# Layer norm issued inside the chunk, K evacuation on ScalarE, and per-tile waits in the first down projection of a retention + mixture-of-experts layer

## The reference, cut to what matters

```python
# attention half (retention): no softmax, a decay mask per head
xn = layernorm(x)                               # (8, 4096, 1024)
Q, K, V = (einsum('bld,hde->bhle', xn, W) for W in (Wq, Wk, Wv))   # 16 heads of 64
scores = einsum('bhle,bhme->bhlm', Q, K) * decay[None] / sqrt(64)
out = einsum('bhlm,bhme->bhle', scores, V)
c = (out - mean(out, per batch, head)) / sqrt(var(out, per batch, head) + 1e-5)
x = x + (c * gn_weight + gn_bias) @ Wout
# expert half: 8 experts, two weighted per token, and a shared one with a sigmoid gate
xn = layernorm(x)
combine = normalised top-2 of softmax(xn @ gate_w.T)               # (tokens, 8)
out = sum_e combine[:, e] * ((silu(xn @ w_gate[e]) * (xn @ w_up[e])) @ w_down[e])
out = out + sigmoid(xn @ shared_gate_w.T) * ((silu(xn @ sw_gate) * (xn @ sw_up)) @ sw_down)
x = x + out
```

## Time and profile before

| what | us |
|---|---|
| median of 2 runs | 6181.56 |
| lowest of them | 5938.66 |
| highest of them | 6424.45 |
| the profiled execution | 5941.39 |
| its span, slowest core (core 1) | 5939.8 |
| span of the shortest core (core 5) | 5902.1 |
| PE busy, core 1 | 5018.9 (84% of the span) |
| ACT busy, core 1 | 1474.9 (25%) |
| DVE busy, core 1 | 1392.0 (23%) |
| mean granted clock of PE, core 1 | 0.905 |

### The profile page before, as it was taken

One profiled execution on the slowest core, in us unless ns is written; L12 is line 12 of the kernel. 1 busy time (PEld: TensorE's weight loads), 2 busy tenths in 40 slices (PEclk: granted clock), 3 DMA queues, 4 the chain that ended last, 5 costly groups with the idle time before them and its releaser, 6 DMA issues.

```text
span 5939.8 us, 65663 instructions; the slowest of 8 cores (5902.1 to 5939.8 us)
## 1 busy us (share of the span) xinstructions
PE 5018.9 (84%) x24644; PEld 2336.3 (39%) x24644; DVE 1392.0 (23%) x3537; ACT 1474.9 (25%) x3619; POOL 159.2 (3%) x279
## 2 busy tenths in 40 slices
PE   3555555589998999899989998999899989998999
PEld 1333333234443444344434443444344434443444
DVE  1334444421112111211121122112211221122111
ACT  2334444231213121312131213121312131213121
POOL 0000000000000000000000000000000000000000
PEclk9666666689998999899989999999899989998999
DMA  9888886224343434343434343434242434242423
GB/s 177 196 211 192 198 204 153 90 85 168 125 156 114 168 125 156 114 168 125 156 114 172 120 161 117 167 117 169 112 164 117 166 118 161 117 168 93 163 117 131
DMA packets 105892, 867.80 MB, mean 146 GB/s; under 512 B 10480, under 2 KB 18672, under 8 KB 74352
## 3 DMA queue, kind: packets, MB, share of 16 engines
q0 software_dynamic: 71728, 786.99, 40.3%
q1 hardware_dynamic: 33856, 76.62, 4.0%
HBM read 838.43 MB, written 103.02 MB: 158 GB/s over the span
## 4 chain that ended last, share of the span: by engine, by line
PE 69%; DMA 5%; ACT 3%; DVE 1%; issue 1%; ACTq 0%; POOL 0%; DVEq 0%; SPq 0%; POOLq 0%
PE psf L972 23%; PE psf L976 23%; PE psf L1029 20%; DMA wring<-wbf 5%; PE psf L837 2%; ACT silu_sb L988 1%; ACT xln_bf L164 1%; PE psb L758 1%; DMA x_sb<-x 1%; ACT ucp_sb L989 1%; DVE h_sb L998 0%; DVE combT L768 0%; DVE xln2T L772 0%; ACT L154 0%; ACT sqdump L133 0%
## 5 line engine op out<-in xcount | busy, mean ns | idle before, releaser
L1029 PE MATMUL psf<-wring,h_sb 128*128 128x512 bf16 x6336 | 1452.9, 393 | 153.1 <-DVE h_sb L998 153.1
L972 PE MATMUL psf<-xln2T,wring 128*128 128x512 bf16 x6336 | 1510.1, 381 | 11.4 <-DMA wring<-wbf 10.7
L976 PE MATMUL psf<-xln2T,wring 128*128 128x512 bf16 x6336 | 1503.6, 380 | 0.0
L988 ACT ACTIVATE silu_sb<-psf 128x512 bf16<-128x512 f32 x792 | 472.9, 597 | 3293.9 <-PE psf L976 3293.8
L1029 PEld LDWEIGHTS psf<-wring,h_sb 128*128 128x128 bf16 x6336 | 633.2, 101 | 972.8 <-issue 285.5
L972 PEld LDWEIGHTS psf<-xln2T,wring 128*128 128x128 bf16 x6336 | 620.7, 98 | 769.0 <-issue 33.1
L976 PEld LDWEIGHTS psf<-xln2T,wring 128*128 128x128 bf16 x6336 | 622.1, 98 | 755.2 <-issue 13.4
L998 DVE TENSOR_TENSOR h_sb<-silu_sb,ucp_sb 128x512 bf16<-128x512 bf16 x792 | 337.0, 425 | 2443.3 <-ACT ucp_sb L989 2443.3
L1045 DVE SCALAR_TENSOR_TENSOR x_sb<-psf,c_sb,x_sb 128x512 f32<-128x512 f32 x576 | 432.7, 751 | 1108.2 <-PE psf L1029 1108.2
L989 ACT CAST ucp_sb<-psf 128x512 bf16<-128x512 f32 x792 | 459.5, 580 | 0.0
L448 PE MATMUL psf<-qt_sb,kt_sb 64*128 64x128 bf16 x512 | 76.4, 301 | 225.1 <-DMA kt_sb<-kt_sb 224.1
(11 more groups left out here) (102 smaller groups left out, 1852.0 us busy)
## 6 DMA issues: line engine op xcount, KB each, us to landing
wring<-wbf POOLq DMA_DIRECT2D x216, 2816.0 KB, 12.4
wbf<-stg POOLq DMA_DIRECT2D x27, 2816.0 KB, 9.5
x_sb<-x SPq DMA_DIRECT2D x64, 512.0 KB, 6.7
stg<-wg POOLq DMA_DIRECT2D x8, 2816.0 KB, 22.4
stg<-wu POOLq DMA_DIRECT2D x8, 2816.0 KB, 23.2
stg<-wd POOLq DMA_DIRECT2D x8, 2816.0 KB, 22.8
out<-x_sb SPq DMA_DIRECT2D x32, 512.0 KB, 15.1
comb<-comb_sb SPq DMA_DIRECT2D x32, 256.0 KB, 7.7
```

The costliest lines, as they stand in the source:

```text
L972: t.matmul(gb, wring[:, wg0 + dt * IFF + it * C:wg0 + dt * IFF + (it + 1) * C], xln2T[:, dt * SC:(dt + 1) * SC], start=(dt == 0), stop=(dt ...
L976: ins = t.matmul(ub, wring[:, wu0 + dt * IFF + it * C:wu0 + dt * IFF + (it + 1) * C], xln2T[:, dt * SC:(dt + 1) * SC], start=(dt == 0), st ...
L988: sc.activation(silu_sb[:, (it % 2) * SC:(it % 2 + 1) * SC], gb, AF.Silu)
L1029: ins = t.matmul(db, h_sb[:, hb + it * SC + tloc * C:hb + it * SC + (tloc + 1) * C], wring[:, wd0 + it * D + dc * 512:wd0 + it * D + (dc + ...
```

## The change

Three things are changed.

1. The layer norm of chunk c is put into the queues in the iteration of chunk c itself, behind everything of chunk c-1 in ACT's queue; the one ahead of the loop goes, and so does the second buffer `xln2b`. The load of x for chunk c+1 still waits for the layer norm of chunk c.
2. The K groups are evacuated by ACT (`sqkv`) and no longer by DVE.
3. In the down projection, the first group waits tile by tile: before matmul `it` for tile `it` of `h_sb`. The wait for the whole of `h_sb` moves to the second group, where it always holds by then.

```diff
-        xln2b = sb1("xln2b", [C, 4 * D], BF16)
@@
         em("sync", ldx0)
-        xtgt0 = S("sld").n
-        em("scalar", lambda sc, tgt=xtgt0: (sc.wait_ge(S("sld").h, tgt), sc.drain()))
-        ln_tgts = {0: emit_ln_sc(x_sb, xln_bf)}
@@
-        xln_bufs = [xln_bf, xln2b]
         for c in range(nsc):
             if use_conv:
                 emit_conversions(4)
+            xtgt = S("sld").n
+
+            em("scalar", lambda sc, tgt=xtgt: (sc.wait_ge(S("sld").h, tgt), sc.drain()))
+
+            ln_done = emit_ln_sc(x_sb, xln_bf)
 
             if c + 1 < nsc:
                 S("sld").n += 64
 
-                def ldx(s, c=c, vtgt=ln_tgts[c], tgt=S("sld").n):
+                def ldx(s, c=c, vtgt=ln_done, tgt=S("sld").n):
@@
                 em("sync", ldx)
-                xtgt = S("sld").n
-                em("scalar", lambda sc, tgt=xtgt: (sc.wait_ge(S("sld").h, tgt), sc.drain()))
-                ln_tgts[c + 1] = emit_ln_sc(x_sb, xln_bufs[(c + 1) % 2])
@@
-            emit_t512a(xln_bufs[c % 2], xlnT, wait_sem="sc1", wait_tgt=ln_tgts[c])
+            emit_t512a(xln_bf, xlnT, wait_sem="sc1", wait_tgt=ln_done)
@@
-                if kind in ("q", "k"):
-                    def vqkv(v, kind=kind, idx=idx, bk=bk, tgt=S("peq").n):
+                if kind == "q":
+                    def vqkv(v, idx=idx, bk=bk, tgt=S("peq").n):
                         v.wait_ge(S("peq").h, tgt)
-                        dst = (qt_sb if kind == "q" else kt_sb)[:, idx * SC:(idx + 1) * SC]
-                        ins = v.tensor_copy(dst, bk)
+                        ins = v.tensor_copy(qt_sb[:, idx * SC:(idx + 1) * SC], bk)
@@
-                    def sqkv(sc, idx=idx, bk=bk, tgt=S("peq").n):
+                    def sqkv(sc, kind=kind, idx=idx, bk=bk, tgt=S("peq").n):
                         sc.wait_ge(S("peq").h, tgt)
-                        tt, ec = idx // 2, idx % 2
-                        dst = v_sb[:, tt * D + ec * 512:tt * D + (ec + 1) * 512]
+                        if kind == "k":
+                            dst = kt_sb[:, idx * SC:(idx + 1) * SC]
+                        else:
+                            tt, ec = idx // 2, idx % 2
+                            dst = v_sb[:, tt * D + ec * 512:tt * D + (ec + 1) * 512]
                         ins = sc.copy(dst, bk)
@@
                             if didx == 0:
-                                t.wait_ge(S("vch").h, htgt)
                                 t.wait_ge(S(ldd[0]).h, ldd[1])
                                 if e == 0:
                                     t.wait_ge(S("scr").h, sctgt)
+                            elif didx == 1:
+                                t.wait_ge(S("vch").h, htgt)
                             if banktgt >= 1:
                                 t.wait_ge(S("vcd").h, banktgt)
                             for it in range(NIT):
+                                if didx == 0:
+                                    t.wait_ge(S("vch").h, htg[it])
                                 ins = t.matmul(db,
```

More of the change, by code:

```diff
@@ L303, in ldx0 @@
             for tt in range(4):
-                ins = s.dma_start(out=x_sb[:, tt * C * 0 + tt * D:(tt + 1) * D],
+                ins = s.dma_start(out=x_sb[:, tt * D:(tt + 1) * D],
                                   in_=x_h[tt * C:(tt + 1) * C, :])
@@ L382, in build_nc @@
                     evac_tgts.append(("vcq", S("vcq").n))
[L383 to L386, removed]
+                    q_evac[idx] = ("vcq", S("vcq").n)
                     em("vector", vqkv)
                 else:
-                    def sqkv(sc, idx=idx, bk=bk, tgt=S("peq").n):
+                    def sqkv(sc, kind=kind, idx=idx, bk=bk, tgt=S("peq").n):
                         sc.wait_ge(S("peq").h, tgt)
-                        tt, ec = idx // 2, idx % 2
-                        dst = v_sb[:, tt * D + ec * 512:tt * D + (ec + 1) * 512]
+                        if kind == "k":
[3 more added lines that the diff above has]
+                            dst = v_sb[:, tt * D + ec * 512:tt * D + (ec + 1) * 512]
                         ins = sc.copy(dst, bk)
@@ L396, in build_nc @@
                     evac_tgts.append(("scq", S("scq").n))
+                    if kind == "k":
+                        k_evac[idx] = ("scq", S("scq").n)
                     em("scalar", sqkv)
@@ L956, in build_nc @@
                 hb = (e % 2) * NIT * SC
+                h_tgts = {}
                 for it in range(NIT):
@@ L1002, in build_nc @@
                     S("vch").n += 1
+                    h_tgts[it] = S("vch").n
                     em("vector", vh)
@@ L1018, in tdown @@
                                   htgt=h_done, ldd=piece_tgt[p0 + 2], hb=hb,
+                                  htg=dict(h_tgts),
                                   banktgt=(S("vcd").n - 1 if (e > 0 or didx >= 2) else -1),
```

## The result

The changed kernel is 1.95% faster: the ratio of its time to that of the kernel before is 0.9805, with a 95% interval of 0.9789 to 0.9820. Its profiled execution took 5817.9 us, the one before 5941.4. It is within a us or two of what the second rival gave, 5819. The sign was wrong, and so was the reason given against that rival.

The account below looks back on a forecast made before the run. Phase 1 was taken as bound by its serial chunks, phase 2 by PE with a gap per expert and weight loads close behind. 5941.4 + 102.4 (phase 1) - 80 (phase 2) = 5964 us, range 5885 to 6050.

Parts of the forecast that it names:

- the second rival: Phase 2: weight requests don't bind, cores drift apart, slowest core's L falls to 16.4; 5819 us; chance 0.04 under 5822.
- Layer norm exposed: Phase 1 chunk starts: Q starts 18.9 us later in seven chunks, +132.3 us.
- one chunk out of the conversions' way: Phase 1, chunk 6: starts after POOL's conversions end, 45.0 instead of 74.9 us to its first L448, -29.9 us.
- The fifth rival: Phase 1 loses nothing, something else filling the 18.9 us: 5861 us; chance 0.03.
- K on ACT: Phase 1 K evacuation: 584 instead of 692 ns each, copies start 0.1 us earlier; taken as zero.
- The down gap: Phase 2, before each down stage: PE's 2.12 us wait for the last h_sb tile, 153.1 us in 72 gaps, goes.
- The slow starts of the down stage: Phase 2: 44 of 72 down stages start at PE's lower clock, 1.69 us each, 74 us; taken as gone.
- L: Phase 2: landing time of the second gate/up weight load; core 1's mean of 18.5 us was used for the changed kernel.
- the ring: Phase 2 weight loads, requested after an expert's last pair: the next gate can't start before U + 2.53 + L.
- the other end: Phase 2: short-L cores run ahead, core 1 comes to the partners' mean 17.9; -121 us instead of -66.
- U: Phase 2: the time at which PE ends an expert's last pair, from which the next gate's start is counted.
- The slow starts before the gate: Phase 2: waits for weight loads drop PE's clock before 41 x 0.61 gates at 1.69 us each, +42 us.

Follow-up runs that it names:

- the layer norm alone: Kernel before with only the layer norm of each chunk issued in its own iteration, one buffer: 6030.6, 6036.2 and 6038.0 us, ratio 1.0144.
- the later and earlier requests: Kernel before plus tile-by-tile down wait, next expert's gate/up weights requested after the first down group (5776.4 us) or once PE ends the last pair (5683.2 to 5694.5 us).

## Why the prediction was wrong

**Phase 1 was right by its own steps.** Layer norm exposed: 7 x 18.9; one chunk out of the conversions' way: -29.9; sum +102.4. The first phase 2 load is 101.6 us later between the slowest cores, and the layer norm alone gives 6036 where 6043 was expected. The waits of L256 are 30.6 us: that is 18.9 and the 9.30 and 2.44 us for which PE stood still there before (the 2.44 in the earlier trace rows), which my 28 had left out. 6 waits on the copies are left of 7, as forecast. The mean over the eight cores is a little more, 1245 instead of 1135 us. The fifth rival, that phase 1 loses nothing, is out.

**K on ACT** at zero: within what could be measured, but only beside the first part; alone it costs 50 to 60 us. The step was right and its condition ("its layer norm is over before Q begins") carried it.

**The down gap** was slightly undersized. I read 2.12 us from the profile's idle time; the distance from a gate start to the down start fell from 40.27 to 37.99 us in the median, so the gap was worth 2.28: 164 us in 72 experts instead of 153. The slow starts of the down stage are gone, all of them, as forecast: 1379.6 us busy for the 1379 foretold.

**The step that failed** is the one that took the landings of the kernel before over into the changed one: "After the change it is the larger of 19.0 and 2.53 + L. With core 1's L of 18.5 that is 21.0". The formula is right, and the later and earlier requests confirm the ring as what holds the gates; the L in it was wrong. L is no property of a core. It changed with the distance between the two cores of a pair, and that distance could change as soon as one of them had to wait. I saw that "cores with a short L run ahead", and gave it as the other end, but then only averaged L between the partners, as though they drifted through all distances, and I rejected the second rival with "one core is enough to hold the time up". No core holds it up: the waiting core is pushed back until it hardly waits any more. With L at 17.0 instead of 18.5 the formula gives 19.5 us from U to the gate, which is about what the changed kernel shows from the down start to the gate (19.4 to 19.6 on the slower partners, 19.2 to 19.3 on the others).

**The slow starts before the gate**, 41 x 0.61 x 1.69 = 42 us in the sum, fell away with it, since few waits are long. Where there are long waits the term is real and larger than I had it: with a wait of 3.7 us, nearly every gate started slow.

**Phase 2 added up again** with what was measured: 72 x 2.28 = 164, 44 slow starts x 1.69 = 74, less the 12 us by which the waits grew, is 226; 225.0 were measured.

The second rival's mechanism, cores moving apart and L falling, is the one that the runs show, and its numbers were nearly right as well: it put the slowest core's L at 16.4 us and the gate at 19.2 us after the last pair, and on core 5 they were 16.6 and 19.3 over the 64 pairs that a gate can wait for (the 17.0 of the table holds the seven pairs at a tile's end too, whose loads take longest). That the sum came out within 2 us all the same is in part luck, and the rival did not say why the cores should move apart.

The Trainium skill ("HBM Reference", Specifications) states that the two cores of a pair share one memory domain. The trace agrees as far as it goes: it is in the pairs 0 and 1, 2 and 3, 4 and 5, 6 and 7 that the distances settle. Of L the runs show means of 16.2 to 16.4 us on the core whose loads come first and of 18 to 19 on its partner while the two are close. The rate of 425 GB/s for a core alone that the same section of the Trainium skill gives, which would be 13.6 us for the two loads (an estimate), was reached by no pair: the shortest L of all runs is 15.2 us, on core 5 of the kernel before, below the 15.6 that I had named as the least. What no run shows is the meeting itself, for the cores' clocks can't be set against each other; that the loads are slower because they meet fits all of this and stays argued.

## What to carry to other kernels

A latency measured where nothing waits for it must not be put into the sum of a kernel in which something will: ask whom the new wait pushes, and where he ends up. With cores that seem to share a resource and run the same loop, such a wait tended here to move them out of each other's way; without one the long landings lasted for the whole run at no visible cost. And a serial chain of small transfers, each waiting for the last, is worth looking for before anything around it is moved, above all where other traffic makes each of them slow: here it held some 150 us, more than the whole change brought.

## What the runs showed of the hardware

- PE's clock fell after idle times of 2.1 us in 44 of 72 cases (the kernel before, core 1). Of 1988 waits before a gate in nine traces, none of the 1404 shorter than 1.96 us was followed by a fall, all of the 344 longer than 3.2 us were, and 190 of the 240 in between. Each fall cost about 1.69 us, eight matmuls of 128x512 at the lower of its two levels.
- The second of two loads of 2816 KB landed in 16.2 to 16.4 us in the mean on the core of a pair whose loads came first, and in up to 19.3 us in the mean on its partner. The difference vanished within some eight experts in the changed kernel, after some thirty where the waits were fewest (the earlier request), and lasted for most of phase 2 in the kernel before, where a long landing was hidden.
- A step of two copies of 64 KB from partition to partition took about 7 us in the mean in a chain while the conversions ran. Issued without a wait between them, all sixteen were done by the end of V, 26 us after the first was issued.
